# A decoder layer on one core: row-chunked first weight merge, a reordered self-attention step, another opening of cross-attention, two tiles' butterflies on the vector engine

## The reference

```python
# self-attention: 16 heads of 128, one shared key/value head, window 128, a sink per head
q = h @ wq_comp @ wq_up                                   # (b, t, 16 * 128)
q = _rmsnorm(_apply_partial_rope(q, cos, sin), q_norm_w)
k = _rmsnorm(_apply_partial_rope(h @ wk, cos, sin), k_norm_w)
v = h @ wv
scores = where(causal and within 128, q k^T / sqrt(128), -1e30)
probs = softmax(concat([scores, sink]))
attn = probs[..., :t] @ v
x = einsum('btgi,gio->btgo', attn, out_w1).reshape(b, t, G * INTER); x @ out_w2
# cross-attention: 16 query heads of 32 on 4 key heads, 1024 keys, ALiBi slopes, mask
w = softmax(Q K^T / sqrt(32) + m * (key - query) masked); out = (w @ V) @ Wo
# feed-forward: 8-bit activations, ternary weights, a Hadamard transform ahead of w_down
gate, up = bitlinear(x, w_gate), bitlinear(x, w_up)       # (2048 wide)
h_bitlinear(silu(gate) * up, w_down)                      # fwht over 2048, then absmax quantisation
```

## Time and profile before

| | us |
|---|---|
| median of 3 runs | 1746.03 (1744.24 to 1747.74) |
| the profiled execution | 1742.52 |
| its span | 1740.7 |
| PE busy in the span | 1632.4 (94%) |
| ACT, DVE, POOL busy | 1238.6, 1202.6, 1184.2 |

### The profile page before, as it was taken

The page is one execution under the profiler, slowest core; times in us unless marked ns, Lnnn a source line. Parts: engine busy times, 40 slices in busy tenths (PEclk is TensorE's granted clock), DMA queues, the critical chain, the costliest instruction groups (busy, mean ns, idle before and its releaser), DMA issues. The chain is left out here.

```text
span 1740.7 us, 24610 instructions
## 1 busy us (share of the span) xinstructions
PE 1632.4 (94%) x7920; PEld 1147.5 (66%) x7920; DVE 1202.6 (69%) x2284; ACT 1238.6 (71%) x2022; POOL 1184.2 (68%) x1085
## 2 busy tenths in 40 slices
PE   6999989999999997799999999999999977999996
PEld 3488878888888875566656665666556534666664
DVE  2378778677766665668787778777787735777764
ACT  2366577888666653589788778888897845787875
POOL 0377877777887762457666666666776739888892
PEclk9999999999999998899999999999999999999999
DMA  6214234333300102411141113101200320001000
GB/s 231 97 61 87 98 104 123 103 94 115 110 13 7 37 7 51 132 42 34 28 122 46 34 34 115 28 28 40 60 24 25 140 109 1 26 26 36 25 20 25
DMA packets 57215, 110.32 MB, mean 63 GB/s; under 512 B 9180, under 2 KB 13660, under 8 KB 56704
## 3 DMA queue, kind: packets, MB, share of 16 engines
q1 hardware_dynamic: 55536, 107.84, 20.1%
q10 hardware_dynamic: 1552, 0.91, 0.2%
HBM read 71.10 MB, written 18.88 MB: 52 GB/s over the span
## 5 line engine op out<-in xcount | busy, mean ns | idle before, releaser
L1351 POOL TENSOR_TENSOR x_p_lo<-x_p,x_p_hi 128x1024 fp32r<-128x1024 f32 x192 | 455.3, 2385 | 232.8 <-ACT x_p_hi L1148 232.4
L1286 DVE TENSOR_REDUCE x_maxes<-x_ps_a 128x1 f32<-128x1024 f32 x252 | 306.9, 1218 | 150.8 <-PE x_ps_a L1435 145.8
L1121 ACT ACTIVATE x_p<-x_ps_b,x_any_valid 128x1024 f32<-128x1024 f32 x256 | 285.1, 1114 | 128.8 <-PE x_ps_b L1418 113.7
L1418 PE MATMUL x_ps_b<-x_Q,x_K 100*128 100x512 f32 x512 | 228.1, 527 | 7.0 <-ACT x_p L1121 4.4
L1148 ACT ACTIVATE x_p_hi<-x_p 128x1024 fp32r<-128x1024 f32 x192 | 203.2, 1058 | 4.8
L1435 PE MATMUL x_ps_a<-x_K,x_Q 99*128 99x512 f32 x504 | 165.9, 410 | 11.2 <-DVE x_maxes L1286 9.0
L1464 PE MATMUL x_ps_o<-x_p_hi,x_V 128*96 128x512 f32 x384 | 156.7, 408 | 1.2 <-POOL x_p_lo L1351 1.2
L1418 PEld LDWEIGHTS x_ps_b<-x_Q,x_K 100*128 100x128 f32 x512 | 89.9, 191 | 99.8 <-issue 74.4
L1465 PE MATMUL x_ps_o<-x_p_lo,x_V 128*96 128x512 f32 x384 | 151.1, 393 | 0.0
L442 ACT ACTIVATE a_work<-a_ps_s,a_neg_max,a_q_r 128x256 f32<-128x256 f32 (+1 forms) x256 | 134.1, 540 | 4.6 <-DVE a_neg_max L542 4.6
L634 POOL TENSOR_TENSOR a_work<-a_work,a_inv_den 128x1024 f32<-128x1024 f32 (+1 forms) x64 | 110.0, 1719 | 18.6 <-DVE a_inv_den L582 18.6
(11 more groups left out here) (254 smaller groups left out, 4353.3 us busy)
## 6 DMA issues: line engine op xcount, KB each, us to landing
shared<-in_L_attn_out_w SPq DMA_DIRECT2D x8, 1024.0 KB, 7.3
shared<-in_L_ffn_w_gate SPq DMA_DIRECT2D x16, 512.0 KB, 4.3
shared<-in_L_ffn_w_up SPq DMA_DIRECT2D x16, 512.0 KB, 4.1
shared<-in_L_ffn_w_down SPq DMA_DIRECT2D x16, 512.0 KB, 4.0
shared<-in_ctx SPq DMA_DIRECT2D x8, 1024.0 KB, 7.5
x_scratch<-rows SPq DMA_DIRECT2D x31, 256.0 KB, 2.0
x_Q<-x_q_hi SPq DMA_DIRECT2D x112, 64.0 KB, 2.0
ffn_quant<-shared SPq DMA_DIRECT2D x24, 256.0 KB, 4.6
```

What stands on the lines that cost most here:

```text
L1121: act.activation(p[:, r, :, :], ps_b[:, :, :], ACT.Exp, scale=any_valid[:, b % 2:b % 2 + 1]).then_inc(exp_ready, 1)
L1286: dve.tensor_reduce(out=maxes[:, c % 2, 32 * r + 3:32 * r + 4], in_=scores_bank(n)[:, :, :], axis=mybir.AxisListType.XY, op=ALU.max).then_ ...
L1351: pool.tensor_tensor(out=p_lo[:, r], in0=p[:, r], in1=p_hi[:, r].bitcast(F32), op=ALU.subtract).then_inc(lo_ready, 1)
L1418: last = pe.matmul(ps_b[:, j, :], K[0:ROWS + 4, g, kb * P:(kb + 1) * P], Q[0:ROWS + 4, hh, :], start=True, stop=True)
```

## The change

- **Merge.** Group 0's weights come as four row chunks (a chunk is 128 rows of each matrix, 256 KB each), with a semaphore each; PE takes the four heads chunk by chunk at c = -8, ahead of its wait for the constants. Then two heads at each of c = -7 to -2. The DMAs of SP stand in another order, and two pairs of `split_part` two steps later.
- **The step.** PE makes the values product of c-2 right behind the scores, in place of c-1 at the end, and the output product at the end. ACT rounds `aT_hi` right before `qT_hi`, and `pT_hi` behind the exponentials. DVE makes `aT_lo` and `neg_r` ahead of `qT_lo`, and `pT_lo` last. POOL takes the power `q_r` last.
- **The opening of cross-attention.** One query bank ahead of the units, the other in quarters beside the first units; heads 0 and 1 prepared on the spot, so that the first spread is six DMAs in place of nine; the tokens of the next sequence are loaded earlier, and its statistics one head later. POOL's cast of the slope rows (L1342) waits for the last of DVE's work on the mask. `slope_columns` is a reduction in place of a copy.
- **Feed-forward.** For tiles 0 and 15 the second `between_quarters` and both `between_halves` stand on DVE.

What is moved is shown where it now stands (the place that it left is named above).

```diff
         def merged_heads(c):
-            return range(2 * (c + 8), 2 * (c + 8) + 2) if -8 <= c < 0 else []
+
+            return range(4) if c == -8 else range(2 * (c + 9), 2 * (c + 9) + 2) if -8 < c < -1 else []
...
-            load_merge(0)
+            for k in range(DC):
+                sp.dma_start(w1_raw[:, 0, k, :], w1t[0, k * P:(k + 1) * P, :]).then_inc(w12_chunk_in[k], 16)
+                sp.dma_start(w2_raw[:, 0, k, :], w2[k * P:(k + 1) * P, :]).then_inc(w12_chunk_in[k], 16)
+            load_merge(1)
             for m in range(3):
                 sp.dma_start(raw_part(m), parts[m][0]).then_inc(part_in[m], 16)
-            load_merge(1)
+            load_merge(2)
+            load_x(1)
             for m in range(3, 7):
                 sp.dma_start(raw_part(m), parts[m][0]).then_inc(part_in[m], 16)
-            for t in range(1, XR1):
+            load_x(2)
+            load_merge(3)
+            for t in range(3, XR1):
                 load_x(t)
...
-                for m in {-7: (0, 1, 2), -6: (3, 4), -5: (5, 6)}.get(c, ()):
+                for m in {-7: (0, 1, 2), -4: (3, 4), -3: (5, 6)}.get(c, ()):
...
+                if 0 <= c - 2 < STEPS:
+                    k = c - 2
+                    act.wait_ge(a_made, k + 1)
+                    act.activation(aT_hi[:, k % 2, :], ps_a[:, :], ACT.Copy).then_inc(aT_hi_ready, 1)
                 if 0 <= c + 1 < STEPS:
                     k = c + 1
                     act.wait_ge(qT_made, k + 1)
                     act.activation(qT_hi[:, k % 2], ps_front[:, :].rearrange("p (a b) -> p a b", a=G1), ACT.Copy).then_inc(qT_hi_ready, 1)
...
                     act.wait_ge(sink_arg_ready, c + 1)
                     act.activation(sink_exp[:, c % 2, :], sink_arg[:, c % 2, :], ACT.Exp).then_inc(sink_exp_ready, 1)
+                if 0 <= c - 1 < STEPS:
+                    k = c - 1
+                    n = len(blocks(k // 4))
+                    act.wait_ge(pT_made, k + 1)
+                    if k:
+                        act.wait_ge(a_made, k)
+                    act.activation(pT_hi[:, 0:n, :], ps_pT[:, 0:n, :], ACT.Copy).then_inc(pT_hi_ready, 1)
...
+                if 0 <= c - 2 < STEPS:
+                    k = c - 2
+                    dve.wait_ge(aT_hi_ready, k + 1)
+                    dve.tensor_tensor(out=aT_lo[:, k % 2, :], in0=ps_a[:, :], in1=aT_hi[:, k % 2, :].bitcast(F32), op=ALU.subtract)\
+                        .then_inc(aT_lo_ready, 1)
                 if 0 <= c + 1 < STEPS:
                     k = c + 1
+                    dve.wait_ge(q_r_ready, k + 1)
+                    dve.tensor_scalar(neg_r[:, k % 4, :], q_r[:, k % 4, :], -1.0, None, ALU.mult).then_inc(neg_r_ready, 1)
                     dve.wait_ge(qT_hi_ready, k + 1)
                     dve.tensor_tensor(out=qT_lo[:, k % 2], in0=ps_front[:, :].rearrange("p (a b) -> p a b", a=G1),
                                       in1=qT_hi[:, k % 2].bitcast(F32), op=ALU.subtract).then_inc(qT_lo_ready, 1)
...
-                    dve.wait_ge(q_r_ready, k + 1)
-                    dve.tensor_scalar(neg_r[:, k % 4, :], q_r[:, k % 4, :], -1.0, None, ALU.mult).then_inc(neg_r_ready, 1)
                 if 0 <= c < STEPS:
                     dve.wait_ge(den_ready, c + 1)
                     dve.reciprocal(inv_den[:, c % 2, :], den[:, c % 2, :]).then_inc(inv_ready, 1)
+                if 0 <= c - 1 < STEPS:
+                    k = c - 1
+                    n = len(blocks(k // 4))
+                    dve.wait_ge(pT_hi_ready, k + 1)
+                    dve.tensor_tensor(out=pT_lo[:, 0:n, :], in0=ps_pT[:, 0:n, :], in1=pT_hi[:, 0:n, :].bitcast(F32), op=ALU.subtract)\
+                        .then_inc(pT_lo_ready, 1)
...
+                if c == -8:
+                    for k in range(DC):
+                        pe.wait_ge(w12_chunk_in[k], 32)
+                        for m in merged_heads(c):
+                            last = pe.matmul(merge_bank(m), w1_raw[:, 0, k, m * P:(m + 1) * P], w2_raw[:, 0, k, :],
+                                             start=(k == 0), stop=(k == DC - 1))
+                            if k == DC - 1:
+                                last.then_inc(w12_made, 1)
+                    pe.wait_ge(const_in, 96)
+                    pe.wait_ge(round_ready, 3)
+                for m in merged_heads(c) if c > -8 else []:
                     g, j = divmod(m, G1)
-                    pe.wait_ge(w12_in[g % 2], 32 * (g // 2 + 1))
+                    pe.wait_ge(w12_in[g % 2], 32 * max(g - 1, 1))
...
+                if 0 <= c - 2 < STEPS:
+                    k = c - 2
+                    blk = blocks(k // 4)
+                    pe.wait_ge(pT_lo_ready, k + 1)
+                    if k:
+                        pe.wait_ge(aT_lo_ready, k)
+                    for kb, slot in enumerate(blk):
+                        last = three(ps_a[:, :], v_hi[:, slot, :], v_lo[:, slot, :], pT_hi[:, kb, :], pT_lo[:, kb, :],
+                                     kb == 0, kb == len(blk) - 1)
+                    last.then_inc(a_made, 1)
...
-                for j in range(1 if b == g == 0 else 0, HPG):
+                for j in range(2 if b == g == 0 else 0, HPG):
...
-            spread_keys(0, 2)
-            spread_keys(0, 3)
-            sp.dma_start(wo_sb[:, :, :], wo.rearrange("(c p) n -> p c n", p=P)).then_inc(wo_in, 16)
             for j in range(2):
                 sp.wait_ge(x1_stored[j], 16 * (TILES // 2))
             sp.wait_ge(first_norm_made, TPB)
             for i in range(TPB):
                 load_x1(1, i)
+            spread_keys(0, 2)
+            spread_keys(0, 3)
+            sp.dma_start(wo_sb[:, :, :], wo.rearrange("(c p) n -> p c n", p=P)).then_inc(wo_in, 16)
...
+            act.wait_ge(first_q_made, 1)
+            for j in range(2):
+                act.activation(Q[0:DH, j, :], ps_j[j * DH:(j + 1) * DH, :], ACT.Copy, scale=QSCALE).then_inc(first_heads_hi_ready, 1)
+            for j in range(2):
+                act.wait_ge(first_heads_hi_ready, j + 1)
+                act.activation(Q[DH:2 * DH, j, :], Q[0:DH, j, :].bitcast(F32), ACT.Copy).then_inc(first_heads_dup_ready, 1)
+            act.wait_ge(first_heads_lo_ready, 2)
+            first_q_hi(0)
...
-                dve.tensor_copy(at[:, :, 0:3], slope_cols[:, c % HX, 0:3].unsqueeze(1).broadcast_to([P, TPB, 3])).then_inc(slope_ready, 1)
+                dve.tensor_reduce(out=at[:, :, 0:3], in_=slope_cols[:, c % HX, 0:3].unsqueeze(1).broadcast_to([P, TPB, 3]).unsqueeze(3),
+                                  axis=AXX, op=ALU.max).then_inc(slope_ready, 1)
...
+                    first = 0 if b else 1
+                    if b + 1 < B and hh == first:
                         statistics(b + 1, r)
-                    if b + 1 < B and (hh, r) == (1, 0):
+                    if b + 1 < B and (hh, r) == (first + 1, 0):
...
+            pool.wait_ge(valid_ready, 1)
...
+                        pe.wait_ge(first_heads_dup_ready, 2)
+                        pe.wait_ge(first_heads_lo_ready, 2)
+                    if n == 8:
...
+                if c == -2:
+
+                    last = pe.matmul(ps_x[:, :], wq_sb[:, r, P:2 * P], hT[:, r, :], start=(r == 0), stop=(r == DC - 1))
+                    if r == DC - 1:
+                        last.then_inc(first_q_made, 1)
...
+        VECTOR_TILES = (0, TILES - 1)
...
+                if i == 0 and quarter(c, 4) and n - 1 in VECTOR_TILES:
+                    between_quarters(dve, n - 1, 2)
+                if i == 1 and quarter(c, 5) and n - 1 in VECTOR_TILES:
+                    between_halves(dve, n - 1, 0)
+                    between_halves(dve, n - 1, 1)
...
-                if i == 0 and quarter(c, 4):
-                    between_quarters(n - 1, 2)
-                if i == 1 and quarter(c, 5):
-                    between_halves(n - 1, 0)
-                    between_halves(n - 1, 1)
+                if i == 0 and quarter(c, 4) and n - 1 not in VECTOR_TILES:
+                    between_quarters(pool, n - 1, 2)
+                if i == 1 and quarter(c, 5) and n - 1 not in VECTOR_TILES:
+                    between_halves(pool, n - 1, 0)
+                    between_halves(pool, n - 1, 1)
                 if i == 2 and quarter(c, 2):
-                    between_quarters(n, 0)
+                    between_quarters(pool, n, 0)
```

180 lines of the change are left out of this document (70 added, 110 removed).

## The result

The changed kernel takes 1721.18 us (1720.2 to 1722.51, 4 runs) against 1745.13 (1744.02 to 1747.74, 4 runs): a ratio of 0.9861, interval 0.9844 to 0.9878, so 24 us or 1.4% faster. I had forecast 1737.5, 8.5 us faster, with 1716 to 1752 as the range. The sign and the range held; the size was off by a factor of three, and the only rival on this side of the forecast, rival 1 (1714), had a chance of 0.15.

The account below looks back on a forecast made before the run. PE bounds the kernel: only less PE work, less idle or an earlier start counts. Terms -9.3 - 1.5 + 11.5 - 6.5 - 1.8 = -7.6 gave 1738.4 on the median, less one for the clock 1737.5; range 1716 to 1752 (8 in 10).

Parts of the forecast that it names:

- rival 1: Self-attention step: the pieces find their bank free, the step gives -10 to -15 us, time about 1714; chance 0.15.
- fill: Pipeline fill: a wait on qT_lo stays, but the new order shortens the others: -1.5 us, bounds 0 and -3.
- the step: Self-attention step: new waits 33 us, neg_r beside POOL 5, old waits gone 26.5, in sum +11.5 us.
- opening: Opening of cross-attention: PE's waits of 5.26 and 1.99 us go, first scores slightly later: -6.5 us, bounds -3 and -10.
- feed-forward: First and last feed-forward tiles: DVE has tile 0's half 2.8 us earlier, tile 15 costs 1: -1.8 us.
- The start: Merge: with chunked weights PE's first matmul comes at 6.1 us, the merge being otherwise the same work: -9.3 us.
- -26.5 at most: Self-attention: PE's idle waits on kT_lo, hT_lo, the values product and the probabilities all go, 26.5 us.
- What comes: Self-attention: pieces wait for qT_lo, 0.45 us each, about 3.0 per 1-block tile and tile behind it: +33 us.
- A cause gone because the output product stands between: Self-attention: the output product, 2.9 us, between piece and next transposes ends the queries' transposes' waits, longest 2.0 us.
- PE is 99% busy, so nothing: Steady cross-attention: the reduction in slope_columns runs beside a PE that is 99% busy, so it gains nothing.
- Tile 15 on DVE: Last feed-forward tile: six operations, 5.4 us of DVE, stand ahead of reads on the last chain and cost 1 us.
- Rival 2: Self-attention: neg_r is caught beside POOL's rotation each time, a term of 19 to 35 us, time say 1757; chance 0.13.

Follow-up runs that it names:

- b_only: The kernel before with the new order of the self-attention step alone, on PE, ACT, DVE and POOL: 1739.19 us against 1742.43, ratio 0.9977.
- negr_late: The changed kernel with neg_r moved behind qT_lo on DVE, nothing else: 1712.56 us against 1742.43 for the kernel before, ratio 0.9821.
- q_first: The changed kernel with qT_hi ahead of aT_hi on ACT, and qT_lo ahead of aT_lo and neg_r on DVE: 1724.45 us, ratio 0.9881 to the kernel before.
- piece_last: The changed kernel with PE's output product put back ahead of the pieces: 1698.37 us against 1744.86 for the kernel before, ratio 0.9733.
- reads_first: The kernel before with aT_hi on ACT and aT_lo on DVE moved behind the reads of the pieces: 1731.53 us against 1740.96, ratio 0.9935.
- a_only: The kernel before with the chunked first merge group alone (chunks, DMA order, later part splits): 1738.84 us against 1742.43, ratio 0.9979.
- c_only: The kernel before with all edits of cross-attention alone: 1727.56 us against 1742.43, ratio 0.9912.
- b_piece_last: The kernel before with the step's new order alone, but the output product ahead of the pieces: 1718.35 us against 1740.96, ratio 0.9857.

## Why the prediction was right or wrong

| term | forecast | measured |
|---|---|---|
| first matmul | -9.3 | -9.3 in the pair of traces; 6.0 to 7.5 us in nine kernels with chunks, 15.1 to 16.8 in five without |
| up to the first scores | 0 | +2.3 |
| fill, behind them | -1.5 | +0.9 (in the next row) |
| the step | +11.5 | -2.1 (trace), -3.2 (b_only, median) |
| opening | -6.5 | -7.6 |
| steady cross-attention | 0 | -3.7 |
| feed-forward | -1.8 | 0.0 (-0.6 and +1.0, with the rest) |

**The step that failed** is the sum of the step, "33 + 5 - 26.5 = +11.5", which measured -2.1 us in the traces and -3.2 in the median of `b_only`; behind it comes the "nothing" for the slope columns, which measured -3.7. From start to start (how much later a matmul begins behind the one before it than the quickest tenth of such pairs in twelve of the traces; an estimate, in us, from step 4 to step 63) the delays of PE are:

| late | before | changed | negr_late | q_first | piece_last | reads_first |
|---|---|---|---|---|---|---|
| queries' transposes | 26.6 | 1.7 | 2.6 | 4.0 | 5.0 | 13.4 |
| probabilities' transposes | 8.1 | 0.1 | 0.1 | 0.1 | 0.1 | 12.5 |
| pieces | 0.1 | 30.6 | 22.4 | 11.8 | 0.4 | 0.1 |
| output product | 1.4 | 2.2 | 2.2 | 22.2 | 9.1 | 1.9 |
| length of the stretch | 530.4 | 528.0 | 520.6 | 533.7 | 509.1 | 521.8 |

- **The start** was right in place and size: 6.1 us forecast, 6.21 measured. What failed is "the merge is otherwise the same work". The first matmuls run at a pitch of 0.86 instead of 0.43 us, six of them here and three in the trace before; over all kernels this slow piece was 3.3 to 6.1 us long, with and without chunks, so it is scatter. It cost 1.2 of the 2.3 us; 0.9 more are idle time ahead of the first scores, on reads by ACT and DVE that didn't move with PE.
- **The fill** I put at -1.5 with the words "shortens the others". The wait of 2.23 us became 3.15, and 4.92 in `a_only`.
- **The step**: as to mechanism, each wait came where I had said, and both sums were mis-sized. "-26.5 at most" is idle time, which counts only part of a delay; from start to start 33 us went. What comes I had counted from start to start, as 38 with `neg_r`; it measured 30.6, some 33 with the first tile. So I set a cost in one measure against a gain in another. Of the 30.6, `neg_r` is 6 to 8 (8.3 us of hold-up, 6.4 of them ahead of a piece that waits; `negr_late` has 8.2 less), for which I had 5 more, and the chain without it 22 to 25, not 33. By tiles the count was close: those with two full neighbours have 1.3 to 1.8, `neg_r` included, against 1.35 and its 0.3; three of the 1-block tiles 2.1 to 2.7 and the four behind such tiles 2.9 to 4.4, against 3.0 and 0.3; but the last two tiles have next to none. In the case at 581 us the transposes begin at 580.65 and `aT_hi` 0.19 later, as counted; the piece could have begun at 582.65 and began 0.33 later, not 0.45.
- **"A cause gone because the output product stands between"** was right in effect and wrong in reason. In `piece_last` the output product does not stand between, and the queries' transposes are late by 5.0 us, not 26.6. `reads_first` shows half of the old delay to be a matter of the order of reads on ACT and DVE, which the change puts right too. So PE's new place for the output product was not needed for this, and it cost 19 to 22 us.
- **The opening** was right in its mechanism and its size within 1.1 us (c_only: 10.3 in the trace, 3.8 more than forecast). The collision of the two casts came as forecast and the first scores 0.9 us later, against 0.6. The rule quoted from the Trainium skill ("SBUF — State Buffer", Terms) is borne out in 27 `neg_r`, 6.37 us of DVE's cast, and the copies.
- **"PE is 99% busy, so nothing"** for the slope columns was wrong by 3.7 us. The wait for the maxima fell by 1.9 us of idle time; the rest of the gain shows in PE's busy time, 690.37 in place of 692.07.
- **Tile 15 on DVE** costs 1.0, as said. Tile 0 gave only 0.6 in this pair of traces, but from the first matmul of the feed-forward to `f_ps_t` of tile 1 the six kernels without DVE's butterflies take 35.5 to 37.8 us and the eight with them 34.0 to 34.9: some 2 us. The two together then come to about -1, not to 0. The part was not run alone.
- **Rival 1** (the piece finds its bank free) lies nearest to what happened, 1714 against 1721, by luck: its condition, that the pieces' waits vanish, did not come true. Rival 2 did not: `neg_r` was caught in 27 of 64.

## What to carry to other kernels

When a bank is reused, count both ways to it: what PE does in between, and what stands ahead of the read in the queues of the reading engines. A short read behind one that waits for PE costs as much as a missing matmul; moving it cost nothing and gave 9 us here. With the new order of reads, the place of one block on PE made 19 to 22 us (`b_only` against `b_piece_last`, the changed kernel against `piece_last`).

A small DVE operation between SBUF operands is priced by what POOL runs beside it and by who waits for it. Take it off the chain, or use a form that isn't held (a reduction for a copy), even where PE seems 99% busy. And where waits go in one place and come in another, take both from the same measure: a gain read from idle time (26.5 here, where 33 went) against a cost counted from start to start made about half of the 14 us by which the sum of the step was off.
